# The second attention's last batch: half of its weighing moves from GpSimd to VectorE, and the feed-forward's statistics move behind the sums

## What is computed

```
x = x + attn_a(layernorm(x))      # 16 heads of 64, causal, over the 256 tokens
x = x + ffn(layernorm(x))         # router, top 8 of 64 slots, GRU, slots' attention
x = x + attn_b(layernorm(x))
x = x + ffn(layernorm(x))

def attn_b(x):                    # N batches, S tokens, H = 16 heads, hd = 8
    q, k, v = (x @ W.T).reshape(N, S, H, hd).transpose(0, 2, 1, 3)   # for Wq, Wk, Wv
    att = softmax(einsum("nqhd,nkhd->nhqk", q, k) / sqrt(hd), axis=3)
    out = einsum("nhqk,nkhd->nqhd", att, v).reshape(N, S, D)
    return out @ Wo.T + bo
```

## Time and profile before

| what | value |
|---|---|
| median of 3 runs | 886.03 us (884.98 to 886.19) |
| the profiled execution's own time | 888.32 us |
| its span, first to last instruction | 886.2 us |
| mean granted TensorE clock | 0.958 |
| busy: PE / PEld / DVE / ACT / POOL | 88% / 68% / 74% / 54% / 47% of the span |

### The profile page before, as it was taken

One profiled execution on the slowest core, in us unless ns is written; L12 is line 12 of the kernel. 1 busy time (PEld: TensorE's weight loads), 2 busy tenths in 40 slices (PEclk: granted clock), 3 DMA queues, 4 the chain that ended last, 5 costly groups with the idle time before them and its releaser, 6 DMA issues.

```text
span 886.2 us, 25741 instructions
## 1 busy us (share of the span) xinstructions
PE 779.7 (88%) x10372; PEld 599.7 (68%) x10372; DVE 652.8 (74%) x1528; ACT 482.5 (54%) x853; POOL 418.3 (47%) x326
## 2 busy tenths in 40 slices
PE   1899999999999999999999896957899999959695
PEld 0688888888888888888888765534455555535554
DVE  3676667666766676677668777635999999998754
ACT  1587668667866686767676452313344444424331
POOL 1354444444444444444446320013898888893000
PEclk9999999999999999999999996988999999977699
DMA  7000000000000000000000000000122222121002
GB/s 292 1 3 1 0 0 0 0 0 0 0 0 0 0 0 0 0 0 0 0 0 3 1 1 1 1 0 1 13 25 24 24 24 24 19 25 18 1 1 95
DMA packets 71589, 13.26 MB, mean 15 GB/s; under 512 B 66432, under 2 KB 70528, under 8 KB 70912
## 3 DMA queue, kind: packets, MB, share of 16 engines
q1 hardware_dynamic: 71552, 12.76, 6.6%
HBM read 8.56 MB, written 4.19 MB: 14 GB/s over the span
## 4 chain that ended last, share of the span: by engine, by line
PE 66%; DVE 15%; ACT 7%; issue 6%; POOL 3%; DMA 2%; DVEq 0%; SPq 0%; ACTq 0%; POOLq 0%
PE PS L572 6%; PE PS L529 6%; PE PS L361 5%; PE PS L362 4%; PE PS L363 4%; PE PS L441 4%; DVE b_prod L895 3%; PE PS L565 3%; PE PS L551 3%; POOL b_w L943 2%; PE PS L780 2%; PE PS L770 2%; DVE a_nm L655 2%; PE PS L967 2%; PE PS L536 2%
## 5 line engine op out<-in xcount | busy, mean ns | idle before, releaser
L688 POOL TENSOR_TENSOR a_pl<-a_p,a_ph 128x1024 f16<-128x1024 f32 (+1 forms) x128 | 210.5, 1645 | 258.9 <-ACT a_ph L601 258.9
L943 POOL TENSOR_TENSOR b_w<-b_v,b_e 128x2048 f32<-128x2048 f32 x32 | 137.9, 4309 | 13.0 <-ACT b_e L861 13.0
L598 ACT ACTIVATE a_p<-PS 128x1024 f32<-128x1024 f32 (+1 forms) x128 | 103.8, 811 | 73.7 <-PE PS L536 73.6
L655 DVE TENSOR_REDUCE a_nm<-PS 128x4 bf16<-128x512 f32 (+1 forms) x128 | 121.4, 949 | 0.1
L591 ACT ACTIVATE a_qk_h<-PS 128x512 f16<-128x512 f32 x128 | 73.4, 604 | 58.2 <-PE PS L363 57.0
L601 ACT ACTIVATE a_ph<-PS 128x1024 f16<-128x1024 f32 (+1 forms) x128 | 103.1, 805 | 0.0
L895 DVE TENSOR_TENSOR b_prod<-PS,b_qt 128x512 f32<-128x512 f32 x128 | 80.3, 678 | 18.3 <-PE PS L772 17.6
L644 DVE TENSOR_TENSOR a_qk_l<-PS,a_qk_h 128x512 f16<-128x512 f32 x128 | 87.0, 681 | 3.4 <-ACT a_qk_h L591 3.4
L384 POOL TENSOR_TENSOR veps<-mv,eps 128x2 f32<-128x2 f32 (+1 forms) x52 | 11.2, 215 | 148.3 <-DVE mv L1244 119.8
L361 PE MATMUL PS<-xhl,a_wqk_h 128*128 128x256 f16 x256 | 71.3, 279 | 8.3 <-ACT xhl L589 7.5
L551 PE MATMUL PS<-a_vh,a_ph 128*128 128x65 f16 x768 | 77.6, 195 | 0.1
(11 more groups left out here) (232 smaller groups left out, 2027.4 us busy)
## 6 DMA issues: line engine op xcount, KB each, us to landing
scratch_dram<-b_o SPq DMA_DIRECT2D x32, 64.0 KB, 4.1
b_y<-scratch_dram SPq DMA_DIRECT2D x16, 128.0 KB, 2.0
out_dram<-X SPq DMA_DIRECT2D x2, 1024.0 KB, 3.9
w_rest<-rest_dram SPq DMA_DIRECT2D x1, 1862.0 KB, 15.2
X<-x_dram SPq DMA_DIRECT2D x1, 1792.0 KB, 11.2
w_first<-first_dram SPq DMA_DIRECT2D x1, 1600.0 KB, 6.9
w_rolls<-rolls_dram SPq DMA_DIRECT2D x1, 544.0 KB, 15.5
X<-x_dram SPq DMA_DIRECT2D x1, 256.0 KB, 3.4
```

Source lines behind the costliest of these rows:

```text
L598: act.activation((a_p0, a_p1)[j][:, me, :, :, :].rearrange("p a h q -> p a (h q)"), TT[:, :, 0:512 - 256 * j], ACT.Exp, scale=EA ** -0.5)
L655: dve.tensor_reduce(a_nm[:, nx, j, :].rearrange("p (a h) -> p a h", a=2)[:, :, 0:2], MM[:, :, 0:256 * (j + 1)].rearrange("p a (h k) -> p a ...
L688: pool.tensor_tensor(*(n[:, g % 2, :, :, :].rearrange("p a h q -> p (a h q)") for n in (pl, p, ph)), ALU.subtract).then_inc(a_split, 1)
L943: pool.tensor_tensor(b_w8[:, j, :, :, :], rolled_values(par, j, 0, H), rolled_exps(par, j, 0, H), ALU.mult).then_inc(b_weighed, 1)
```

## The change

For the last batch alone, the second half of the weighing is made by VectorE ("weigh_last") and summed by it right after ("sum_last"), in the place where GpSimd had its half; "gather" 1 in the epilogue goes. The statistics and first reciprocal roots of the feed-forward (quads 0 to 3) move from behind "sumexp" to behind "gather" 0. All other batches keep their steps.

```diff
@@ b_steps
     put(True, ("weigh", 0))
     put(former, "normal")
-    put(True, ("weigh", 1))
+    put(not tail, ("weigh", 1))
+    put(tail, "weigh_last", "sum_last")
...
     put(True, "sumexp")
-    put(tail, ("ffn_stats", 0), ("ffn_stats", 1), ("ffn_rstd", 0), ("ffn_rstd", 1), ("ffn_stats", 2), ("ffn_stats", 3))
...
     put(True, ("gather", 0))
+    put(tail, ("ffn_stats", 0), ("ffn_stats", 1), ("ffn_rstd", 0), ("ffn_rstd", 1), ("ffn_stats", 2), ("ffn_stats", 3))
@@ B_EPILOGUE
-B_EPILOGUE = [("project", 0, 0), ("finish", 0, 0), ("add", 0, 0), ("yt", 0, 0), ("gather", 0, 1), ("normal", 0, 0),
+B_EPILOGUE = [("project", 0, 0), ("finish", 0, 0), ("add", 0, 0), ("yt", 0, 0), ("normal", 0, 0),
@@ b_vector
+                elif kind == "weigh_last":
+                    dve.wait_ge(b_exped, b + 1)
+                    dve.wait_ge(b_values, b + 1)
+                    dve.wait_ge(b_summed, b)
+                    link(dve.tensor_tensor(b_w8[:, 1, :, :, :], rolled_values(par, 1, 0, H), rolled_exps(par, 1, 0, H), ALU.mult))
+                elif kind == "sum_last":
+                    dve.tensor_reduce(b_s[:, par, 1, :], b_w8[:, 1, :, :, :].rearrange("p h e s -> p (h e) s"),
+                                      X_AXIS, ALU.add).then_inc(b_summed, 1)
```

## The result

The changed kernel takes 888.46 us (median of 12 executions) against 885.96 for the kernel before in the same series: a ratio of 1.0032 [1.0022, 1.0043], or 2.5 us by the medians and 2.8 by the ratio. The forecast was 888.3. A second series gave 1.0028 [1.0017, 1.0040]. One of the 12 executions of the kernel before took 4103.6 us; without it the median is 885.89.

The account below looks back on a forecast made before the run. TensorE was taken to bound the kernel, waiting for batch 14's heads to return from DRAM before the hidden step. The later of the VectorE and GpSimd paths added 2.3 us to 886.03, giving 888.3, range 886.4 to 889.6.

Parts of the forecast that it names:

- The meeting: Batch 15's weighing: VectorE's multiply, both inputs in SBUF, issued at 787.75, waits for GpSimd's weighing and ends at 792.75.
- mirror row: Trace row at 874.44: GpSimd's four-element addition took 0.56 instead of 0.20, ending 0.06 after VectorE's two-input subtraction.
- The VectorE path: Multiply to hidden step: VectorE's normalisings come 5.1 us later, the hidden step 2.2 late at first quad, 2.4 at second.
- The GpSimd path: Batch 14's normalising waits for the multiply, 2.05 us late; its DRAM transfers follow, so the hidden step could start at 803.84.
- "Moved" at nothing: Four statistics and two pairs of reciprocal roots behind the sums: cost nothing, with 2 us of cover for batch 15's transfers.
- The sum: Whole kernel: the later of two paths counts, 2.3 us, added to the median 886.03 for 888.3.
- The last quad's statistics: Feed-forward statistics on VectorE: their 2.6 us wait for batch 15's sum is eaten up; ready near 813.9, 2.4 later.
- no meeting: Rival at the multiply: it does not wait, the first quads are ready just in time, time 886.0; chance 0.08.
- The clock gives it back: Rival in the hidden step: TensorE's clock rise keeps its instant, 1.1 us comes back, leaving 887.2; chance 0.22.

Follow-up runs that it names:

- e2: Changed kernel with the multiply's exponentials read from a second copy that ScalarE writes to PSUM; ratio 0.9990 to the kernel before, 886.11 us against 887.11.
- e3: Changed kernel with the statistics back behind "sumexp" and VectorE's multiply and its sum behind "gather" 0, when GpSimd is idle; ratio 1.0001 to the kernel before, 886.79 us.
- e12: The changed kernel, unaltered, measured again in a later series; ratio 1.0028 to the kernel before, 888.29 us against 886.14.
- e5: Changed kernel with two statistics ahead of the second half's sum and quads 0 and 1 normalised ahead of the last two statistics; ratio 1.0009 to the kernel before.
- e7: The kernel before, unaltered, timed against itself and profiled again; ratio 0.9994, 886.63 us against 887.09.
- e9: Kernel before with 39 tiny fills of an unused tile at the start of VectorE's program; ratio 0.9981, 884.56 us against 886.14.
- e1: Kernel before with only the statistics and roots moved behind "gather" 0, the weighing staying on GpSimd; ratio 0.9975, 884.28 us against 887.11.
- e8: e1 measured again: the kernel before with only the statistics and roots moved; ratio 0.9978, 884.77 us against 887.09.
- e10: e1 with 27 tiny fills at the start of VectorE's program; ratio 0.9989 to the kernel before, 884.54 us against 886.14.
- e6: Kernel before with batch 14's normalising on GpSimd ahead of the first half of batch 15's weighing; ratio 0.9983, 885.44 us against 887.09.
- e4: e2 with the multiply made twice into the same place; ratio 1.0016 to the kernel before, 888.62 us against 887.11.
- e11: e2 with e6's early normalising, e5's early normalisings of quads 0 and 1, and the multiply behind two statistics; ratio 1.0015 to the kernel before, 887.31 us.

## Why the prediction was right, and where it was so by luck

**The meeting: right.** The multiply started at 787.13 and ended at 791.92, 2.16 after GpSimd's weighing (forecast 2.14). Alone it takes 2.28 to 2.29 (e2, e3), so it stood still for 2.5. (The forecast's 2.29 was read from L1393, which is a subtraction and not a multiply; it held.) GpSimd's normalising did wait for it, as taken from the mirror row, and ended 0.49 after it (forecast 0.50): at 7.60 after E against 5.55 before, 2.05 later (forecast 2.05). So here the VectorE instruction that waited got in ahead of the next one in GpSimd's own order, in all three profiles with the meeting (2.67 to 2.68 us, changed kernel, e12, e5). The Trainium skill's rule ("SBUF — State Buffer", "Who interferes with whom"), that the two exclude each other, holds at this size: 4.79 us in place of 2.29; and with one input in PSUM, where the rule has no lock, 2.29.

**The VectorE path: right.** The hidden step came 2.27 later from E (2.08 against e7's profile; forecast 2.2 to 2.4), with a wait for normalised tiles ahead of it (0.71, in e12 0.87): of the two paths, which the forecast had within 0.2 us of each other, this one ended last by that much.

**The GpSimd path: half right.** The normalising was 2.05 late as worked out, but the transposes 1.35, since the store took 4.49 us. The step "the two DRAM transfers move with it" carried 5.14 us over as if it were the store's own; 0.65 of it went with the packet of VectorE's program, and is gone where that packet falls elsewhere (e9).

**"Moved" at nothing: right in its stretch, not in the times.** The statistics' new place was costed by the cover of batch 15's transfers. That held (its transposes at 811.31 don't wait). But the kernel with the move alone is about 2 us faster (e1, e8), and the sum has no term for that. The edited stretch shows little of it: from E to the start of the last output products e1 takes 89.98 us and e8 90.43, the kernel before 90.43 in e7's profile and 92.25 in the first. That is at most 0.45 against e7's, although the hidden step, behind a shorter store, starts 0.7 earlier. Another part lies ahead of E, before anything that the edit moves. E in e1's profile and in e8's, two of one kernel:

```profile
783.43 0.60 ACT L861 ACTIVATE b_e<-PS 128x512 f32<-128x512 f32 x1 [1.70 <-PE PS L761]
785.60 0.60 ACT L861 ACTIVATE b_e<-PS 128x512 f32<-128x512 f32 x1 [1.71 <-PE PS L761]
```

These two profiles are together at 501.1 (GpSimd's last L688) and 1.8 us apart at attention b's first products (L895, 595.7 and 597.5); in between, from 583.5 to 587.5, TensorE's clock is at 1.2 GHz in e8's and at 2.4 GHz in e1's. The mean granted clock of an execution is at least 0.961 in 21 of 23 executions of e1 and e8 (e1's profiled one 0.963, e8's 0.959) and in 11 of 12 of e9, but in 11 of 97 of the kernel before. So the gain goes, for a good part, with the clock of earlier stages. Why a move in the tail, or fills at the start, should go with that clock is open.

**The sum: right in its stretch, and by luck to a few tenths in the times.** From E to the last output products the changed kernel takes 93.23 us, and 93.07 in e12. That is 2.6 to 2.8 more than e7's profile of the kernel before, 0.8 to 1.0 more than the first profile (whose stretch at 1.2 GHz is spoken of below), and 2.8 to 2.9 more than e2 (90.29), which has the same order and the same multiply without a meeting. So the meeting costs there the sum's 2.3 and some 0.5 more, which is the size of the clock's part estimated below; and without the meeting nothing is lost (e2 against e1 and e8: -0.1 to 0.3), as the rival "no meeting" had it.

The whole times say something else. Against the order alone the change costs 3.5 to 4.2 us by the medians (4.4 to 5.1 by the ratios), and e2 stands 1.8 above e1. In the profiles of these two a difference of that size lies ahead of E (785.55 against 783.43) and hardly any behind it; e2's mean clock reached 0.961 in 3 of 11 executions, e1's in 10 of 11. So the 3.5 to 4.2 can't be called the price of the meeting. The measured 2.5 against the kernel before holds two things, too, that no term of the sum stands for: the 0.5 outside the span, and an E that comes 0.8 to 1.3 earlier in the two profiles of the changed kernel than in the two of the kernel before. They have opposite signs, so that 888.3 came so close to 888.46 is in part luck.

**The last quad's statistics** wait 0.86 for batch 15's residual sum (2.64 before), where the forecast had that wait eaten up.

**The clock gives it back: refuted.** The rival had the rise keep its instant. By windows of half a microsecond the clock rose 22.7 us after E in the changed kernel (22.5 in e12), against 19.1 and 19.7 in the two profiles of before: 2.8 to 3.6 later, more than the hidden step. It rose 4.3 us after that step began (4.1 in e12), before 2.9 and 3.3; so about a microsecond more of it ran at 1.2 GHz. A pair of router products takes 1.97 us at that level and 1.07 at the other, so that is an estimated 0.5 us on top of the shift. That the wait is the reason isn't shown: in e8, without any wait, it rose 4.3 after the step began as well. Windows after:

```profile
804.00:806.00 2.00, 2.00 (x7) 1.00 (x6) 2.00 (x9) 1.27 (x3) 0.27 (x1) 0.50 0.44 31
...
816.00:818.00 2.00, 1.75 (x16) 1.51 (x15) 1.70 (x10) 0.84 (x2) 0.26 (x1) 1.00 0.00 0
```

The low stretch at 816 is gone, but it is absent in e7's profile of the kernel before as well: that difference, which hides the loss in the spans, belongs to the execution and not to the change.

**Faster than both kernels** are the order alone (884.3 and 884.8, against 887.1), the two padded kernels (884.6 and 884.5 against 886.1) and the early normalising (885.4 against 887.1). In none of them does the multiply leave GpSimd; e2, where it does, is 1.0 faster by the medians, but its interval reaches 1.0000.

## What to carry to other kernels

A VectorE instruction with two SBUF inputs, laid beside a long GpSimd instruction, paid twice here: it waited for that one, and GpSimd's next waited for it. Give it one input from PSUM, or a place where GpSimd is idle. Before a duration is carried over to the new place, ask what else was in it: a small transfer on the path may hold a fetch of another engine's program (5.14 us in place of 4.50 here), and 39 idle instructions that moved that program went with a gain of 1.7 us, where the edit cost 2.5. Compare stretches from a common event, and take a second profile: the same tail took 92.25 and 90.43 us in two of the kernel before, and the common event itself stood 2.2 us apart in two of e1's kernel. A variant's whole time may thus hold gains of stages that it doesn't edit; look for them before giving them to the edit.

## What the runs showed of the hardware beyond that

- One packet of VectorE's program, inside a store of two tiles, went with 5.14 and 5.39 us in place of 4.48 to 4.50; at the store's first moment, with 4.87; with its last data (e3), with 4.49.
- From TensorE's restart (the transposes of batch 14) to the rise of its clock to 2.4 GHz it took 4.1 to 7.5 us where the hidden step doesn't wait (before 5.9, e7 6.3, e1 6.9, e8 7.5, e5 4.7, e9 4.1, e10 6.3), 7.1 and 7.4 with waits of 0.22 and 0.29 ahead of it (e2, e3), 8.2 and 8.1 with 0.71 and 0.87 (changed kernel, e12), 9.3 with 2.23 (e6), 10.9 with 2.67 (e4), and 12.7 with 0.68 and another 0.71 inside (e11). On the whole a longer wait went with a later rise; that it is the cause was not separated.
- In the first profile of the kernel before the clock fell to 1.2 GHz at 814.9, with TensorE's matmuls busy in all of every half microsecond from 799 to 815; in e7's profile, with the same instructions, it stayed at 2.4 GHz there.
- The time outside the span is a matter of the program: 2.0 to 2.2 us in every execution of the kernel before, 2.5 to 2.7 in the changed kernel and e3, 1.8 to 1.9 in e5, e9, e10 and e11. What sets it was not looked into.
